# A transformer kernel on one core: band queries and keys projected once, their halves swapped on VectorE, the bias on ScalarE, and PSUM banks given out singly

## The reference, cut to what matters

```python
q = _apply_rope(proj(Wq, bq))      # y = x @ W.T + b, 1024 features
k = _apply_rope(proj(Wk, bk))
v = proj(Wv, bv)
...
def _apply_rope(x):
    x1, x2 = jnp.split(x, 2, axis=-1)            # halves of one head: 32 + 32
    rot = jnp.concatenate([-x2, x1], axis=-1)
    return x * cos + rot * sin
...
valid = band[None] & ((nidx > 0) | (kj[None] >= W))     # W = 128
attn = jax.nn.softmax(scores, axis=-1)
return merged @ Wo.T + bo
```

## Time and profile before

| | us |
|---|---|
| median of three runs | 2152.45 |
| lowest, highest | 2148.47, 2153.92 |
| profiled execution, its own time | 2152.07 |
| its span, first to last instruction | 2150.2 |
| mean granted TensorE clock | 0.936 |
| PE, DVE, ACT, POOL busy | 1789.7, 1345.8, 808.8, 978.6 |

### The profile page before, as it was taken

The page is one execution under the profiler, slowest core; times in us unless marked ns, Lnnn a source line. Parts: engine busy times, 40 slices in busy tenths (PEclk is TensorE's granted clock), DMA queues, the critical chain, the costliest instruction groups (busy, mean ns, idle before and its releaser), DMA issues.

```text
span 2150.2 us, 51747 instructions
## 1 busy us (share of the span) xinstructions
PE 1789.7 (83%) x21261; PEld 1250.9 (58%) x21261; DVE 1345.8 (63%) x2753; ACT 808.8 (38%) x1303; POOL 978.6 (46%) x1362
## 2 busy tenths in 40 slices
PE   4899889999999998879999997777776778888883
PEld 4566565666666666655555555667665455555553
DVE  4555555555555543574555555677876788888873
ACT  2333333333333332324444444333333444444441
POOL 3333222333332222453333435689997455555543
PEclk9999999999999999989999999888998788888886
DMA  4000000000000000023333332233443223323310
GB/s 161 1 1 1 1 2 1 1 1 1 1 1 1 1 1 1 16 56 74 64 78 71 75 75 61 60 74 78 91 87 65 46 62 65 65 65 65 65 21 8
DMA packets 167465, 89.54 MB, mean 42 GB/s; under 512 B 9393, under 2 KB 165810, under 8 KB 166978
## 3 DMA queue, kind: packets, MB, share of 16 engines
q1 hardware_dynamic: 167010, 85.70, 18.4%
q0 software_dynamic: 224, 0.54, 0.1%
HBM read 46.36 MB, written 39.85 MB: 40 GB/s over the span
## 4 chain that ended last, share of the span: by engine, by line
PE 51%; DVE 27%; ACT 7%; POOL 7%; issue 6%; DVEq 0%; POOLq 0%; ACTq 0%
PE slots L1327 38%; DVE nmx L1201 12%; PE ctx_ps L1327 10%; DVE rope_part L1242 4%; ACT probs L1087 3%; DVE rope_part L1166 2%; PE slots L1615 2%; ACT ctxT L1007 1%; DVE ctxT L1303 1%; DVE rope_part L1167 1%; POOL xn L922 1%; PE slots L1394 1%; ACT band_va L1023 1%; POOL band_rb L645 1%; DVE band_r L1167 1%
## 5 line engine op out<-in xcount | busy, mean ns | idle before, releaser
L1087 ACT ACTIVATE probs<-slots 128x1024 f32<-128x1024 f32 (+1 forms) x416 | 356.1, 892 | 322.0 <-PE slots L1327 318.8
L1201 DVE TENSOR_REDUCE nmx<-slots 128x8 f32<-128x1024 f32 (+2 forms) x352 | 407.7, 1216 | 102.8 <-PE slots L1327 101.2
L1327 PE MATMUL slots<-band_r 64*64 64x64 bf16 (+4 forms) x5120 | 393.6, 263 | 80.5 <-DVE nmx L1201 41.7
L1327 PEld LDWEIGHTS slots<-band_r 64*128 64x128 bf16 (+2 forms) x5120 | 194.6, 120 | 254.3 <-issue 129.8
L1242 DVE SCALAR_TENSOR_TENSOR rope_part<-slots,bias_qk,rope_band 128x256 f32<-128x256 f32 x512 | 212.3, 477 | 197.3 <-PE slots L1327 176.4
L1327 PE MATMUL ctx_ps<-probs,band_va 64*32 64x64 f32 (+4 forms) x5120 | 260.5, 313 | 42.3 <-issue 19.4
L986 POOL TENSOR_TENSOR band_r<-rope_part 128x512 f32<-128x512 f32 x128 | 164.5, 1285 | 250.9 <-DVE rope_part L1242 250.9
L1327 PE MATMUL slots<-mask,ident_bf 128*128 128x256 bf16 (+1 forms) x896 | 217.2, 324 | 46.9 <-DVE nmx L1201 17.7
L1327 PE MATMUL slots<-nmT,pick 64*128 64x256 bf16 (+2 forms) x2560 | 218.7, 241 | 2.7 <-issue 2.7
L1327 PEld LDWEIGHTS ctx_ps<-probs,band_va 128*32 128x32 f32 (+2 forms) x5120 | 145.3, 118 | 125.6 <-issue 62.8
L900 POOL TENSOR_TENSOR var_eps<-mean_var,eps 128x2 f32<-128x2 f32 x128 | 29.2, 228 | 393.4 <-DVE mean_var L1129 393.4
(11 more groups left out here) (181 smaller groups left out, 2947.5 us busy)
## 6 DMA issues: line engine op xcount, KB each, us to landing
band_r<-scratch SPq DMA_DIRECT2D x192, 192.0 KB, 4.5
scratch<-parts SPq DMA_DIRECT2D x96, 192.0 KB, 2.2
scratch<-parts SPq DMA_DIRECT2D x96, 128.0 KB, 2.1
scratch<-parts SPq DMA_DIRECT2D x96, 64.0 KB, 1.8
x<-in_x SPq DMA_DIRECT2D x16, 128.0 KB, 4.5
out<-x SPq DMA_DIRECT2D x16, 128.0 KB, 1.8
band_r<-in_band_qk_a SPq DMA_DIRECT2D x1, 1024.0 KB, 6.4
band_va<-in_band_qk_b SPq DMA_DIRECT2D x1, 1024.0 KB, 10.3
```

The costliest lines, as they stand in the source:

```text
L1087: nc.scalar.activation(probs[:, g % 2, step[2], :, 0:width], slot(u, step).rearrange("p (a n) -> p a n", a=2)[:, :, 0:width], ACT.Exp, sca ...
L1201: nc.vector.tensor_reduce(dst, src, axis=AX.X, op=ALU.max, negate=True).then_inc(free_sem(u, step), 1)
L1327: return nc.tensor.matmul(o, lhsT, rhs, start=start, stop=stop, skip_group_check=shared)
```

## The change

In the band layer a chunk's queries and keys are projected once, 6 matmuls instead of 12, into one bank. The features of a head are laid out so that the two halves of each pair sit 16 lanes apart inside a group of 32 partitions. The work after PE is split anew. ACT adds the bias, out of PSUM into `biased`, one activation each for queries and keys. POOL multiplies `biased` by the cosine (`cos`). DVE swaps the halves with a lane permutation of `biased` into `turned` and multiplies that by the sine (`sin`). POOL adds the two products, and the cast stays as it was. The four matmul products on DVE are gone. The weights and biases are half as large, and so are their loads and splits in the setup.

The six banks are given out singly. A step that fills at most 512 columns (`narrow`) takes one bank, the others take a pair, each bank and pair with a semaphore of its own. `LEAD` and `PER_UNIT`, the numbers that rank the steps, are new throughout, so the order of all layers moves.

```diff
 SLOTS = 3
+BANKS = 2 * SLOTS
...
-                steps.append(("qk", j))
+                steps += [("qk", j), ("cos", j), ("sin", j)]
...
-        "qk": [("pe", 1.43), ("dve", 1.56), ("pool", 1.21)] if big else [("pe", 0.72 if low else 1.43)],
+        "cos": [("pool", 1.21)],
+        "sin": [("dve", 1.3), ("pool", 1.21)],
+        "qk": [("pe", 0.72), ("act", 0.74)] if big else [("pe", 0.72 if low else 1.43)],
...
     "pe": {
...
-        "maxima": {"band": 15.183, "causal": -0.256, "chunk": 0.135, "lowrank": -1.548},
+        "maxima": {"band": -19.457, "causal": 0.831, "chunk": 3.799, "lowrank": 0.687},
...
+def narrow(kind, step):
+    name = step[0]
+    if name == "v":
+        return kind != "band"
+    if name == "qk":
+        return kind in ("band", "lowrank")
+    if name == "ffn":
+        return step[1] == 2 and AHEAD[kind] == "ffn0"
+    return name in ("xT", "down", "nm", "den", "rden", "ctx", "ctxT", "out")
...
+                    if step[0] == "cos":
+                        j = step[1]
+                        c = b * CHUNKS + j
+                        if c >= 2:
+                            pool.wait_ge(band_sum, c - 1)
+                        pool.wait_ge(biased_ready, c + 1)
+                        released(pool, u, ("qk", j))
+                        nc.gpsimd.tensor_tensor(rope_part[:, c % 2, 0], biased[:, c % 2], rope["band"][:, 0:1, :].to_broadcast([P, 2, TOK]),
+                                                ALU.mult).then_inc(cosine_ready, 1)
+                    if step[0] == "sin":
+                        j = step[1]
+                        c = b * CHUNKS + j
+                        pool.wait_ge(cosine_ready, c + 1)
+                        pool.wait_ge(sine_ready, c + 1)
...
+                        act.wait_ge(front_full, FRONT_NO[u, step] + 1)
+                        for qk in range(2):
+                            nc.scalar.activation(biased[:, c % 2, qk], slot(u, step)[:, TOK * qk:TOK * (qk + 1)], ACT.Identity,
+                                                 bias=bias_qk[:, j, qk:qk + 1]).then_inc(free_sem(u, step) if qk else biased_ready, 1)
...
-                        for rot in range(2):
-                            for qk in range(2):
-                                o = 512 * qk + TOK * rot
-                                nc.vector.scalar_tensor_tensor(
-                                    rope_part[:, c % 2, rot, qk, :], slot(u, step)[:, o:o + TOK],
-                                    bias_qk[:, j, 2 * qk + rot:2 * qk + rot + 1], rope["band"][:, rot, :],
-                                    ALU.add, ALU.mult).then_inc(part_ready, 1)
...
+                        nc.vector.stream_shuffle(turned[:].rearrange("p q n -> p (q n)"),
+                                                 biased[:, c % 2].rearrange("p q n -> p (q n)"), HALVES_SWAPPED).then_inc(turn_ready, 1)
+                        dve.wait_ge(turn_ready, c + 1)
+                        nc.vector.tensor_tensor(rope_part[:, c % 2, 1], turned[:], twice(rope["band"][:, 1, :]), ALU.mult).then_inc(sine_ready, 1)
...
                         if kind == "band" and name == "qk":
-                            for i in range(4):
+                            for i in range(2):
                                 last = mm_split(F[:, i * TOK:(i + 1) * TOK], [w[:, step[1], i, :] for w in band_qk], [v[:] for v in xT_attn])
```

More of the change, by code:

```diff
@@ L289 @@
 WAKE = {"pe": 0.05, "act": 0.03, "dve": 0.03, "pool": 0.07, "sp": 0.1}
+HALVES_SWAPPED = [(i + 16) % 32 for i in range(32)]
 LEAD = {
     "pe": {
[L294 to L297 removed]
@@ L298 @@
-        "maxima": {"band": 15.183, "causal": -0.256, "chunk": 0.135, "lowrank": -1.548},
-        "back": {"band": -2.437, "causal": -0.43, "chunk": -0.634, "lowrank": -1.541},
+        "tail": {"band": 10.921, "causal": 51.656, "chunk": 8.997, "lowrank": 1.163},
+        "finish": {"causal": 0.073, "chunk": -0.104, "lowrank": 1.066, "end": 0.825},
+        "forward": {"causal": 29.99, "chunk": 5.788, "lowrank": 2.502, "end": 0.875},
+        "operands": {"band": 6.672, "causal": 21.495, "chunk": 20.79, "lowrank": 16.432},
@@ L306 @@
-        "back": {"band": 0.035, "causal": -3.733, "chunk": 11.32, "lowrank": 7.631},
+        "tail": {"band": -72.927, "causal": 6.274, "chunk": 19.296, "lowrank": 50.309},
+        "finish": {"lowrank": 56.005, "end": -34.044},
+        "forward": {"causal": 92.35, "chunk": 4.041, "lowrank": 16.71, "end": 68.449},
+        "operands": {"band": 7.705, "causal": -55.171, "chunk": -85.53, "lowrank": 11.32},
+        "back": {"band": -6.726, "causal": -34.568, "chunk": 15.619, "lowrank": 11.13},
@@ L307 @@
     },
     "dve": {
[L309 to L313 removed]
+        "tail": {"band": -1.972, "causal": 60.023, "chunk": -1.841, "lowrank": -26.695},
@@ L314 @@
+        "finish": {"causal": -68.655, "chunk": -1.927, "lowrank": 2.834, "end": 10.857},
+        "forward": {"causal": 31.589, "chunk": 64.033, "lowrank": 34.654, "end": 7.535},
+        "operands": {"band": -1.574, "causal": 2.152, "chunk": -0.802, "lowrank": 22.039},
+        "maxima": {"band": 33.06, "causal": 28.058, "chunk": 5.326, "lowrank": 20.155},
     },
     "pool": {
-        "tail": {"band": 8.427, "causal": 6.479, "chunk": -24.474, "lowrank": 9.213},
-        "finish": {"causal": -25.627, "chunk": -19.656, "lowrank": -10.06, "end": 52.839},
@@ new lines @@
+        "operands": {"band": -37.238, "causal": -24.568, "chunk": 69.868, "lowrank": -40.662},
+        "maxima": {"band": 31.045, "causal": -1.925, "chunk": 69.815, "lowrank": 16.586},
+    },
+}
+PER_UNIT = 0.0056
+def narrow(kind, step):
[7 more added lines that the diff above has]
+    return name in ("xT", "down", "nm", "den", "rden", "ctx", "ctxT", "out")
@@ L422, in make_plan @@
         if eng == "pe" and step[0] in FRONT_FILLS + BACK_FILLS:
-            slots[u, step] = slot, len(held[slot])
-            held[slot].append(released_by(u, step))
+            if narrow(UNITS[u][0], step):
+                free_now = [i for i in range(BANKS) if at[i] < UNKNOWN and at[i] + WAKE["pe"] <= start]
+                first = max(free_now, key=lambda i: (at[i ^ 1], -i))
+                taken, sem = [first], SLOTS + first
+            else:
+                first = min(range(0, BANKS, 2), key=lambda i: (max(at[i], at[i + 1]), i))
+                taken, sem = [first, first + 1], first // 2
+            waits = {held[i]: None for i in taken if held[i] is not None}
+            slots[u, step] = first, sem, counts[sem], tuple((slots[fill][1], slots[fill][2] + 1) for fill in waits)
+            counts[sem] += 1
+            for i in taken:
+                held[i] = u, step
         free[eng] = start + time
```

126 lines of the change are left out of this document (65 added, 61 removed).

## The result

The median of 8 runs is 2141.1 us (2139.65 to 2146.4), that of 8 runs of the kernel before beside them 2152.7 (2148.47 to 2157.23). The ratio is 0.9948, with a 95% interval of 0.9934 to 0.9961: the change gains 0.5%, 11.6 us, where 60 were forecast. The direction was right, the size a fifth of the forecast.

A forecast was written before the change was run, and what follows sets the result against it. PE was taken to bound the band layer (94% busy). From the 2150.2 us span, -30 periods, -8 weights, -5 units 1 and 2, +3 setup and unit 0, -20 later gave 2090, forecast as a 2092 us median; range 2035 to 2145.

The forecast's parts named there:

- Matmuls removed: Band-layer projection on PE: half of a chunk's matmul time, 0.75 us, goes; 6.0 us a unit, 96 us over 16 units.
- The work in their place: Band layer: DVE's swap and product, 0.69 us each; ACT's two copies, 0.75 us; one more POOL operation, 1.285 us a chunk.
- The pitch: Time from chunk to chunk on POOL: about 3.0 us, as DVE and POOL block each other; bounds 2.65 and 3.3.
- The period, walked through: Schedule of one band unit: 48.7 us, or 46.2 without the clash of DVE and POOL; 48.0 was taken.
- The sum: Terms against the 2150.2 us span: periods -30, weights -8, units 1 and 2 -5, setup with unit 0 +3, later -20.
- Units 1 and 2, -5: The two band units said to lie ahead of the 12 counted periods: 5 us saved.
- Behind unit 12, -20: Last three band units and three later layers: -20 us of 1386 from order and single banks; bounds +20 and -55.
- The clock: Granted clock in the band layer: PE 87% busy at a period of 48 us; nothing charged for a fall.
- (a): PE stays the bound of the band layer, no clash that matters: period 44 to 45.5 us, total 2044; chance 0.25.
- (b): DVE and POOL lock each other out fully in the band layer: pitch 3.3, period 50, total 2121 us; chance 0.18.
- (c): POOL's chain bounds the band layer: at pitch 3.6 us the period is 51.5, total 2174 us; chance 0.09.
- (d): The removed matmul work is hidden anyway and nothing moves; chance 0.03.

## Why the direction was right and the size wrong

**Matmuls removed**: right in kind. A chunk costs 0.80 us at the full clock (2.39 for three) and 0.89 on average in the band layer, where 0.75 was forecast and 1.55 was measured before. The group takes 115.0 us over the run where "about 100" was forecast.

**The work in their place**: the swap (0.74 for 0.69) and ACT's pair (0.84 for 0.75) were near. The product at 0.69 was right only where no POOL operation runs beside it (in the run without the cosine product its median is 0.69 and its mean 0.81); with the block it took 1.04 to 1.79.

**The pitch**: right, 3.03 us against 3.0. "POOL hides some 0.2 of it in its own start" was an estimate near the mark: the earlier trace rows give 0.14 (the cast ends 0.10 us behind DVE's product and takes 0.236 alone), and the changed kernel shows 0.14 on either side. The Trainium skill, SBUF — State Buffer, section Who interferes with whom, says that the lock on the shared ports is exclusive and that whichever of the two starts first makes the other wait. The trace agrees: each operation ends a fixed time behind the other's end, and 3.3 is missed because 0.14 us of each start lies outside the wait.

**"The period, walked through"** is the step that failed, in what it made of the pitch. Held against the unit at 474.43: maxima end at 14.7 (14.6 forecast), `sum` 3 at 19.8 (19.3), `out` starts at 27.2 (26.5) and takes 0.5 us longer at the lower clock, and the rest of the round behind `v` 1 is 17.4 instead of 16.7, since PE waits 0.97 us for POOL's tokens at 460.84. That is 50.4 where the walk has 48.7, and the text then took 48.0, because "overlaps give some back". They did not: DVE is in one piece from the first score fill on. The 2.4 us a period that the forecast missed are thus 0.7 ahead of `out`, 0.5 of clock, 0.7 of waiting for tokens and 0.7 taken off for overlaps, less 0.3 in `v`. The walk also hung the piece on POOL alone ("five sums"), where DVE's swaps, products and `scale` are a chain without a gap, which can set the unit without any block, as the run with the extra product shows. So taking the clash away gives less than was thought: without it the walk gave 46.2, and the two kernels nearest to that (the product ahead of the swap, no cosine product) run at 48.5 and 48.3, some 2 us above. The clash itself was priced at 2.5 us a unit and measured 1.9 (against the product ahead of the swap, where DVE's chunk is 0.3 us shorter) to 2.1 (against the run without the cosine product). "DVE's 1.4 us instead of 1.9, not on the path by itself" was wrong twice: with the block and the gaps it is 2.1, and it is on the path.

**The sum**, term by term. Periods and weights, -38 forecast: -10.3 measured, of which the weights are 7.9 as forecast (8) and the plain units 2.4 instead of 30. "Units 1 and 2, -5" was counted twice, as they lie behind 142.72 already. Setup and unit 0, +3: +4.6 (PE begins 2.2 us earlier at 14.85, the first projection 2.9 earlier at 30.23, and from there to the first score it is 27.9 us where 26.7 was forecast and before had 20.6). Behind unit 12, -20: -4.0, where the banks alone give -17. Together -9.7, which is the difference of the spans.

**The clock**, charged at nothing: it fell in two of eleven 5-us windows of the unit, behind PE's waits for DVE there, and holding it up gave 0.7 us a unit. "If it falls, that speaks for c" did not hold: it fell with the pitch at 3.03.

**Rivals**: (a), a period of 44 to 45.5, and (b), a pitch of 3.3, didn't come. (c) had POOL's chain as the bound of the band layer, from a pitch of 3.45 on; the bound came at 3.03, as the chain that DVE and POOL make together, and 5.5 us per us is near what DVE's time per chunk costs from 1.76 us on. (d), nothing moves, had the least chance, 0.03, and by number it came nearest, though the removed work wasn't hidden: PE waits for DVE in its place. That the range of 2035 to 2145 held the 2141 is luck: its upper end was set to leave out (c) and a part of (d), not by anything that came to pass.

## What to carry to other kernels

When work leaves the engine that bounds a stage, add up every other engine between the two points of the unit that wait for each other, not over the whole unit: DVE was 57% busy and, but for 0.4 us, had no gap in the 21.5 us that set the period. A DVE product with two SBUF operands beside GpSimd cost 1.5 to 2.6 times its own time (1.04 to 1.79 us for 0.69), and its busy time was partly waiting; moved ahead of the swap so that it reads PSUM, it gave 1.9%. And an order that was searched for one set of durations and resources is part of the kernel: when one of them changes, hold the order to see what the change is worth, as the run with the banks dealt over the old order did.

## What was not expected of the hardware

A lane permutation of 512 fp32 columns over 128 lanes costs 0.74 us, 0.05 more than a product of that width alone, plus 14 ns for its mask. The block between DVE and POOL is exclusive and the same from both sides: a DVE product ends 0.55 us behind POOL's operation, a POOL product 1.13 behind DVE's, each its own time less 0.14. What looks uneven, a cosine product of either 1.27 to 1.30 or 1.71 to 1.75 us and a DVE product of anything from 1.04 to 1.79, is only where each of them begins in the other's turn. And 29 small matmuls of no use, 3.9 us of PE's time in a unit, brought the granted clock from 0.60 and 0.72 back to 1.00 and shortened the unit by 0.7 us.
